# C stored once and B stored by chunk in DRAM, and two barriers replaced by the waits of each reader, in an adaLN, Mamba and expert layer on one core

## The reference, cut to what matters

```
h = _layernorm(x) * (1 + ca) + sa
z = h @ Wz.T + bz
Bm = repeat((h @ WB.T).reshape(b, l, 8, 16), 4)       # 8 heads, each used by 4
Cm = (h @ WC.T).reshape(b, l, 32, 16)                 # 32 heads of 16 states
delta = softplus(h @ Wdt_down.T @ Wdt.T + 2 * bdt)
u = silu(conv(repeat(h @ Wx.T + bx)) + conv_b)
# for each channel and each of the 16 states, over the tokens:
state = exp(-exp(A_log) * delta) * state + delta * u * B
y = sum over the states of state * C
y = (y + u * D) * silu(z)
x = x + ga * (y @ Wout.T + bout)
```

## Time and profile before

| | us |
|---|---|
| median of 3 runs | 943.36 (943.11 to 946.33) |
| the profiled execution | 951.12, its span 949.3 |
| stage A, to the first barrier | 167.5 |
| scan, to the second barrier | 167.5 to 604.4 |
| output projection, routing, experts | 604.4 to 949.3 |

### The profile page before, as it was taken

The page is one execution under the profiler, slowest core; times in us unless marked ns, Lnnn a source line. Parts: engine busy times, 40 slices in busy tenths (PEclk is TensorE's granted clock), DMA queues, the critical chain, the costliest instruction groups (busy, mean ns, idle before and its releaser), DMA issues.

```text
span 949.3 us, 10338 instructions
## 1 busy us (share of the span) xinstructions
PE 749.2 (79%) x2240; PEld 368.4 (39%) x2241; DVE 639.7 (67%) x878; ACT 324.5 (34%) x360; POOL 502.0 (53%) x263
## 2 busy tenths in 40 slices
PE   5888969388878687787878787875329999999995
PEld 2433324132322232222323232564215666666663
DVE  4355662599999999899999999555504444444442
ACT  1564663445444444445444444001011111111110
POOL 1000000399999999999999999414622222222222
PEclk9898988599999998989999899986559999999998
DMA  9354540687877777777777688561361222222220
GB/s 260 96 136 146 131 142 0 174 219 200 220 201 213 185 221 192 200 182 217 209 191 213 185 219 221 183 241 68 113 221 35 42 44 44 44 43 43 43 38 0
DMA packets 75004, 137.05 MB, mean 144 GB/s; under 512 B 11426, under 2 KB 47586, under 8 KB 74852
## 3 DMA queue, kind: packets, MB, share of 16 engines
q1 hardware_dynamic: 64620, 127.97, 48.5%
q0 software_dynamic: 7152, 8.48, 5.3%
q10 hardware_dynamic: 3208, 0.34, 0.3%
HBM read 93.82 MB, written 39.66 MB: 141 GB/s over the span
## 4 chain that ended last, share of the span: by engine, by line
PE 43%; DVE 22%; POOL 10%; issue 10%; DMA 7%; ACT 6%; SPq 2%; ACTq 1%; POOLq 1%; DVEq 0%
DVE pool L1045 16%; PE PS L651 14%; PE PS L667 7%; PE PS L452 7%; PE PS L553 6%; ACT PS L800 4%; POOL pool L1310 4%; DMA C_scratch<-Y 4%; PE PS L584 3%; POOL spread L1333 3%; POOL expert_in_scratch L1360 2%; PE PS L659 2%; DVE pool L1033 2%; PE PS L535 1%; PE PS L639 1%
## 5 line engine op out<-in xcount | busy, mean ns | idle before, releaser
L1310 POOL TENSOR_TENSOR pool<-pool,hT 128x1024 f32<-128x1024 f32 x128 | 298.6, 2358 | 21.3 <-PE PS L553 17.4
L553 PE MATMUL PS<-pool,ident 128*128 128x512 f32 x512 | 261.1, 634 | 45.5 <-POOL pool L1310 45.3
L1045 DVE TENSOR_TENSOR_SCAN pool<-PS,pool 128x1024 f32<-128x1024 f32 x96 | 215.7, 2274 | 0.0
L800 ACT ACTIVATE PS<-pool,negA 128x1024 f32 (+1 forms) x128 | 143.1, 1118 | 195.9 <-DVE pool L1045 195.8
L1379 POOL DMA_INDIRECT out<-uT,ptab x39 | 60.6, 1554 | 184.3 <-DVE uT L1256 177.7
L553 PEld LDWEIGHTS PS<-pool,ident 128*128 128x128 f32 x512 | 96.0, 197 | 154.4 <-POOL pool L1310 74.8
L1033 DVE TENSOR_TENSOR pool<-PS,pool 128x1024 f32<-128x1024 f32 x96 | 117.6, 1225 | 40.9 <-PE PS L535 31.6
L651 PE MATMUL PS<-pool,uT 128*128 x312 | 142.6, 600 | 0.8 <-ACT uT L864 0.4
L535 PE MATMUL PS<-pool 96*128 96x512 bf16 x256 | 81.8, 403 | 54.7 <-DVE pool L1033 44.2
L1302 POOL TENSOR_TENSOR pool<-pool,uT 128x1024 f32<-128x1024 f32 (+1 forms) x8 | 18.9, 2359 | 143.0 <-ACTq L790 143.0
L1230 DVE TENSOR_TENSOR uT<-uT,PS 128x512 f32<-128x512 f32 x39 | 26.9, 689 | 92.8 <-PE PS L651 90.0
(11 more groups left out here) (163 smaller groups left out, 699.9 us busy)
## 6 DMA issues: line engine op xcount, KB each, us to landing
hT<-C_scratch SPq DMA_DIRECT2D x128, 512.0 KB, 5.7
expert_in_scratch<-zrow SPq DMA_DIRECT2D x68, 261.0 KB, 5.8
C_scratch<-Y SPq DMA_DIRECT2D x16, 512.0 KB
pool<-in_w SPq DMA_DIRECT2D x16, 512.0 KB, 10.0
uT<-expert_in_scratch SPq DMA_DIRECT2D x39, 130.5 KB, 2.1
Y<-Y SPq DMA_DIRECT2D x32, 128.0 KB, 2.4
Y<-in_wo SPq DMA_DIRECT2D x8, 512.0 KB, 10.5
x_tok<-in_x SPq DMA_DIRECT2D x4, 512.0 KB, 8.9
```

The lines of the kernel that those rows point to most:

```text
L553: m = pe.matmul(PS[:, 6 + half, :], ident[:, :], prod[:, k % PR, HF * half:HF * half + HF], start=False, stop=k == DS - 1)
L800: act.activation(pair(2 * (k % 2)).unsqueeze(1), delta[:, bass.ds(g2 * 2 + r, 1), :], ACT.Exp, scale=decay[:, bass.ds(g2 * (2 * DS) + n, 1 ...
L1045: dve.tensor_tensor_scan(hst[:, k % HR, :], pair(2 * (k % 2)), driven, 0.0, ALU.mult, ALU.add).then_inc(scan_done, 1)
L1310: gp.tensor_tensor(prod[:, k % PR, :], hst[:, k % HR, :], crep[:, k % RC, :], ALU.mult).then_inc(prod_done, 1)
```

## The change

- C is stored once: 8 stores, each of 128 rows. The load of a step takes 8 rows, each for 16 partitions, where it took 16 rows for 8 partitions each.
- B is stored in 4 transfers for each batch, one for each chunk, in place of 3, one for each part.
- `a_over` and `b_over` are gone. SP issues the first load of B after the first chunk of z, the loads of C after the last (they overwrite `hT`); PE waits for what its first `front` reads, POOL for delta and u.
- The remaining four stores of zeros come after the scan's loads.
- ACT makes the decay rates before the loop of stage A, and spreads `sel` after the second silu of z.
- PE does the output projection of tiles 0 and 1 before the last but one `back`, of tile 2 before the last, and goes on with tile 3. DVE's last gate and the tables of the routing come after the first tiles' additions.

```
-            for landed, n in [(B_out, PARTS * (1 + NB) - 1)] + [(o, NB * CH // 2) for o in C_out + C_again]:
+            for landed, n in [(B_out, CH * (1 + NB) - 1)] + [(o, NB * CH // 2) for o in C_out]:
...
-                    for d, landed in enumerate((C_out[c % 2], C_again[c % 2])):
-                        sp.dma_start(C_twice[bass.ds(b * (DIN // DS) + c * HC, HC), d], C_st[:, c % 2, :]).then_inc(landed, 16)
+                    sp.dma_start(C_dram[bass.ds(b * DIN + c * P, P), :], C_st[:, c % 2, :]).then_inc(C_out[c % 2], 16)
...
-                for part in range(PARTS):
-                    sp.dma_start(B_dram[bass.ds(b * CH, CH), part], B_parts[:, part, :]).then_inc(B_out, 16)
+                for c in range(CH):
+                    sp.dma_start(B_dram[bass.ds(b * CH + c, 1)].rearrange("g a i n -> i (g a) n"),
+                                 B_parts[32 * c:32 * c + 32, :, :]).then_inc(B_out, 16)
...
-            sp.wait_ge(a_over, 4)
             sp.sem_inc(stk_free, 1)
             sp.wait_ge(zero_rows, 4)
-            for i in range(NG * 8, NZ):
-                zeros(i)
...
-                                     C_rows[bass.ds((g2 * 2 + r) * 2 * HC, 2 * HC), k, :]
-                                     .unsqueeze(1).broadcast_to([2 * HC, DS // 2, L])).then_inc(crep_in[k % RC], 16)
+                                     C_dram.rearrange("(h s) n -> h s n", s=DS)[bass.ds((g2 * 2 + r) * HC, HC), k, :]
+                                     .unsqueeze(1).broadcast_to([HC, DS, L])).then_inc(crep_in[k % RC], 16)
...
+            sp.wait_ge(z_mm, 1)
             B_of(0, 0)
+            sp.wait_ge(z_mm, NB * CH)
...
-            pe.drain().then_inc(a_over, 1)
-            pe.wait_ge(sel_done, 1)
-            pe.wait_ge(a_over, 4)
+            pe.wait_ge(sel_done, HB)
+            pe.wait_ge(dt_free, 1 + NB * CH)
+            pe.wait_ge(C_copied, 1 + NB * CH)
...
+                if t == 0:
+                    pe.wait_ge(folded, 2)
+                    pe.wait_ge(gated, CH)
+                if t in (0, 2):
+                    pe.wait_ge(scan_done, 2 + NG * DS - (t == 0))
...
+                        if last and r == 1 and k == DS - 2:
+                            outward_y(0)
+                            outward_y(1)
+                        elif last and r == 1 and k == DS - 1:
+                            outward_y(2)
                         back(g2, r, k)
...
             for r in range(2):
                 act.wait_ge(C_out[r], 16 + 16 * NB * CH // 2)
-                act.wait_ge(C_again[r], 16 + 16 * NB * CH // 2)
...
+            for n in range(NB * CH):
+                act.wait_ge(z_mm, n + 1)
+                act.activation(szT[:, n, :], pair(2 * (n % 2)), ACT.Silu, bias=col[:, BZ + n % CH:BZ + n % CH + 1]).then_inc(sz_done, 1)
+                if n == 1:
+                    spread_rows()
```

More of the change, by code:

```diff
@@ L368, in _ @@
             C_of(NG // 2 - 1, True)
-            sp.wait_ge(b_over, 4)
+            for i in range(NG * 8, NZ):
+                zeros(i)
+            sp.wait_ge(ysum_done, RC + NG * DS)
             for dst, src in ((w0_sb, w0), (w1_sb, w1)):
@@ L555, in back @@
                 m.then_inc(ysum_done, 1)
-            def blocks_of(g2, last):
-                for r in range(2):
-                    for k in range(DS):
-                        if k + LAG < DS:
-                            front(g2, r, k + LAG)
-                        elif r == 0 or not last:
-                            front(g2 + r, 1 - r, k + LAG - DS)
-                        back(g2, r, k)
-            for k in range(LAG):
-                front(0, 0, k)
-            with pe.Fori(0, NG // 2 - 1) as g2:
-                blocks_of(g2, False)
-            blocks_of(NG // 2 - 1, True)
-            pe.drain().then_inc(b_over, 1)
-            pe.wait_ge(b_over, 4)
-            pe.wait_ge(folded, 2)
             def outward_y(t):
                 b, at = t // NTB, t % NTB * P
+                if t == 0:
[3 more added lines that the diff above has]
+                    pe.wait_ge(scan_done, 2 + NG * DS - (t == 0))
                 if t == NTB:
@@ L586, in outward_y, with blocks_of @@
                 m.then_inc(o_mm, 1)
+            def blocks_of(g2, last):
+                for r in range(2):
+                    for k in range(DS):
+                        if k + LAG < DS:
+                            front(g2, r, k + LAG)
+                        elif r == 0 or not last:
+                            front(g2 + r, 1 - r, k + LAG - DS)
+                        if last and r == 1 and k == DS - 2:
[3 more added lines that the diff above has]
+                            outward_y(2)
+                        back(g2, r, k)
+            for k in range(LAG):
+                front(0, 0, k)
+            with pe.Fori(0, NG // 2 - 1) as g2:
+                blocks_of(g2, False)
+            blocks_of(NG // 2 - 1, True)
             def turn_h2(t):
@@ L617, in ranks @@
                 m.then_inc(rank_mm, 1)
-            for t in range(TQ):
-                outward_y(t)
+            outward_y(TQ - 1)
             for stage in range(NQ + 3):
@@ L719, in _, with decay_rates @@
             act.wait_ge(mod_step, 2)
+            def decay_rates():
+                act.wait_ge(acol_in, 16)
+                for n in range(NB):
+                    act.activation(negA[:, n, :], acol[:, :, :].rearrange("p c s -> p (c s)"), ACT.Exp).then_inc(col_done, 1)
             for b in range(NB):
+                if b:
+                    decay_rates()
                 for j in range(2):
@@ L773, in _, with spread_rows @@
                 ln_w(3)
-            act.wait_ge(acol_in, 16)
-            for b in range(NB):
-                act.activation(negA[:, b, :], acol[:, :, :].rearrange("p c s -> p (c s)"), ACT.Exp).then_inc(col_done, 1)
-            act.wait_ge(sels_in, 16)
-            for j in range(HB):
-                act.activation(sel[0:PARTS * 32, :, (P // HB) * j:(P // HB) * j + P // HB],
-                               state_rows[0:PARTS * 32, DS * j:DS * j + DS].unsqueeze(2).broadcast_to([PARTS * 32, DS, P // HB]),
-                               ACT.Copy).then_inc(sel_done, 1)
             for r in range(2):
                 act.wait_ge(C_out[r], 16 + 16 * NB * CH // 2)
-                act.wait_ge(C_again[r], 16 + 16 * NB * CH // 2)
-            with act.Fori(0, NB) as b:
-                for c in range(CH):
-                    act.wait_ge(z_mm, b * CH + (c + 1))
-                    act.activation(szT[:, bass.ds(b * CH + c, 1), :], pair(2 * (c % 2)), ACT.Silu,
-                                   bias=col[:, BZ + c:BZ + c + 1]).then_inc(sz_done, 1)
-            act.drain().then_inc(a_over, 1)
-            act.wait_ge(a_over, 4)
+            def spread_rows():
+                act.wait_ge(sels_in, 16)
+                for j in range(HB):
+                    act.activation(sel[0:PARTS * 32, :, (P // HB) * j:(P // HB) * j + P // HB],
+                                   state_rows[0:PARTS * 32, DS * j:DS * j + DS].unsqueeze(2).broadcast_to([PARTS * 32, DS, P // HB]),
+                                   ACT.Copy).then_inc(sel_done, 1)
+            for n in range(NB * CH):
[3 more added lines that the diff above has]
+                    spread_rows()
+            act.wait_ge(col_done, NB + 1)
+            act.wait_ge(d_done, NB)
+            act.wait_ge(sz_done, 2 + NB * CH)
             act.sem_inc(scan_done, 2)
@@ L1183, in _ @@
                         gathered(t)
+                if stage == 0:
+                    gate_y(CH + 3)
+                    route_tables()
                 if 0 <= stage - 3 < NQ - 2:
```

46 lines of the change are left out of this document (18 added, 28 removed).

## The result

The changed kernel took **921.79 us** (median of 4 runs, 920.31 to 923.63), the kernel before beside it 943.57 (943.11 to 946.33, 4 runs): ratio 0.976, 95% interval 0.974 to 0.979. The forecast was 994. The change is faster by 22 us where I had it slower by 51. The profiled spans are 949.3 and 920.4, a difference of 28.9; the kernel before's profiled execution lay 7.6 above the median of its four runs and the changed kernel's 0.4, so about 22 of this are the change. A median is of all runs of a kernel, while a ratio compares only runs within 1.5% of the fastest of their kernel.

The account below looks back on a forecast made before the run. DVE and POOL bound the scan, POOL at 3.25 us a step; the change would make loads the bound at 3.95. The difference, 128 s - 455, gave +50.6 on 943.4: 994 us, range 912 to 1060, the forecast's own 960 to 1040.

Parts of the forecast that it names:

- The scan's loads: Scan: loads of C on 8 of 16 engines take 3.5 us, making a step 3.95 us, bounds 3.05 and 4.55.
- +50.6: Whole kernel: predicted change in us at a step of 3.95 us, added to the median of 943.4.
- the rest that these engines carry: Scan: zeros add 0.40 us and B 0.05 us to each step on the engines that load C.
- The other bound: Scan: POOL's work fills a step of 3.25 us; above that the DMA engines set the pace.
- The bound from below: Scan: a load of C takes at least 2.6 us, at the stores' 203 GB/s on 8 engines.
- Stage A: Stage A: quicker stores of C end z at 146.9 instead of 166.2, 19.3 us less.
- The handover: Between last z and first `front`: without barrier, zeros and load of B there, PE goes on at once, 9.1 us less.
- readers wait as long without the barrier: Rival, handover: the 9.1 us stay; 922 us with hidden loads, 1003 with the forecast's; no separate chance given.
- The first weigh: Scan's start: the first load, issued at 146.9, begins at about 149, and the loads' count starts there.
- my formula: Scan's end: tile 7 ends at 163.6 + 128 s us, s being the step's time; before, it ended at 618.6.
- The tail: Scan's end: output tiles 0 to 2 ahead of the last sums save 5 us if loads hold POOL back, otherwise 2.
- the hidden case: Rival, scan: loads stay hidden at a 3.05 us step, 30.4 us less, 913 us; chance 0.20 for hidden or nearly so.

Follow-up runs that it names:

- the whole burst with zeros between: Changed kernel plus bursts of 32 loads of C before the scan, this one with a store of zeros per two loads: 3.26 us per load.
- the padded kernel: Changed kernel with 64 unused elements added to each row of C in DRAM, so a load's rows lie 68 KB apart: 921.3 us, ratio 0.971.

## Why the prediction was wrong

- **The scan's loads, the step that failed.** "A step costs 3.05, 3.95 or 4.55 us": it cost 3.33. 128 x (3.95 - 3.33) = 79.4 us, and that is the whole distance between +50.6 and -28.9. Two parts. The load was put at 3.5 and is 3.28 alone on average: 0.2 us, within what I had taken as open. The larger one is "to this comes the rest that these engines carry", 0.45 us: the runs with half and twice the zeros (at most 0.09 us in a step), and the whole burst with zeros between (3.26 us for a load and half a store, 3.28 without), show that the zeros don't add. I had added durations of transfers that each run alone on engines that were said to be full. That 3.28 and 3.33 agree is in part luck: the load alone drifted between 3.6 and 3.0 us, one with neighbouring rows cost 4.06 in a burst and 3.50 in the scan, and a load of 2.6 us (68 KB) would have left only the 3.25 of the other engines, but its scan still took 421.0 and not 417. What a load costs inside the scan, beside compute, stays open.
- **The other bound, 3.25 us.** I called it POOL's. In the kernel before POOL's weigh has 4% of the chain and DVE's scan (L1045) 16%; DVE was busy 340.5 us from 200 to 560 and POOL 341.4. The loads come in between these two, now one and now the other ending last, and POOL's tenths stayed at 9 where I had said 7 or 8.
- **The bound from below** (2.6 us, the stores' rate) was real: 2.51 to 2.67 us with the rows 17 or 33 apart. That a load's time hangs on where its rows lie stood nowhere in my working. Neighbouring rows, 64 KB and more took 4.06, 3.14 and 2.6 us, the full range that I had to choose from.
- **Stage A**, -19.3: right in its mechanism, too small. z ended at 139.9, not 146.9. C's last chunk left PE at 112.3; by my steps, the first batch's 7.6 us taken off the second, it would have been 117.1. Most of those 4.8 us are two more chunks at 3.70 in place of 5.40 (at 54.60 and 96.61; the padded kernel, the same in stage A, had 5.40 at 55.48, and its first `front` came at 144.1). The other 2 are ACT's: it began its first silu at once, so PE never waited. Separately, storing C once gave -21.4, B by chunk -16.5, both -25.6 (175.2 to 149.6 with the barrier back): they cure the same wait of DVE and ACT for transfers in one queue. I had costed the two together and could not see that. (One execution each; the long profile of before is worth up to 4 us in the first two and in the last.)
- **The handover**, -9.1: right; 9.34 with the barrier back. The rival "readers wait as long without the barrier" fell.
- **The first weigh.** I let the first load start the count at 149, 2 us after its issue. It was issued at 140.3, and the first weigh came at 149.3: fronts, drives and a scan lie between, in PE's slow clock (0.50 from 147 to 152). This 7 us too few and the front part's 7 us too many cancelled by luck, so my formula, fed with 3.33, gives 163.6 + 426.2 = 589.8 for tile 7, and 589.7 was measured.
- **The tail**, -5: 3.6 in the profiles, nothing in the medians.
- **Which rival came true?** None as written. It is the hidden case's sign with the forecast's mechanism: the eight engines set a part of the pace (the loads 13% of the chain, share 0.58 where I said 0.55, 8.1 to 12.7 us to landing where I said over 10), but at 3.33 us, just under the 3.55 from which it would have cost more than the front gave. I had named that point and given 0.23 to all below it. The chance was wrong because the two ends of the load's price, 2.6 and 4.1, were 1.5 us apart, 190 us in the total, and I took the middle for likely.

The Trainium skill, page "DMA: Bandwidth & Descriptors", section "Why a DMA increments its semaphore by 16 and not by 1", has the rule on the number of engines; it held for the shapes seen here: share 0.50 to 0.51 for eight rows, 1.03 for sixteen. Its section "Specifications" gives about 27 GiB/s for an engine; eight engines came to 209 GB/s at best, 26 GB/s each, and to 129 GB/s, 16 each, with neighbouring rows. In GB/s the page's figure is 29, so it is a ceiling here, which the load came within 10% of or missed by 44%, by where its rows lay.

## What to carry to other kernels

A transfer cut to half the engines need not take twice the time (here 2.15 us became 2.5 to 4.1): price it at the rate that an engine reaches with fewer at work, and where that price decides the sign, the honest forecast has two humps and not a middle. Don't add the durations of transfers that share engines; a run with twice the small ones tells whether they add. And look along a burst before taking its average as a price. And when two edits shorten the same queue, their gains need not add: 21.4 and 16.5 us alone were 25.6 together.

## What the runs showed that I had not expected

- A load of 8 rows, each for 16 partitions, took on average 4.06 us with neighbouring rows, 3.14 to 3.28 with rows 64 KB apart, 2.63 at 68 KB and 2.51 at 132 KB, each time at the DMA share of eight full engines. With 16 rows, neighbouring or 64 KB apart, the scan was the same (418.6 and 417.7 us).
- The DMA share doesn't tell how much room is left: 0.51 stood beside 160 GB/s and beside 209. Judge an engine's room by bytes, not by its busy time.
- The same transfers ran at two speeds in one burst: two loads and a store of zeros took 8.8 us near its start and 5.74 later, where a load with its half of a store (2.87 us) was quicker than the average load alone (3.28). Why is open; that the zeros put the engines out of step is only a guess.
- In kernels with the changed kernel's stage A the first `front` came between 139.3 and 144.3, by whether two chunks of PE after a gap of 2 us took 3.70 or 5.40 us. With none of the two slow it was 139.3 to 140.4, with one 141.0 and 141.1, with both 143.3 to 144.3. A difference of 4 us in one profile is no evidence here.
